# Edge stage: blocks of 128 edges as rows, VectorE adds the second operand, one transpose turns two blocks

## The reference, cut to what matters

```python
pair_emb = jnp.concatenate([node_emb[src], node_emb[dst]], axis=-1)
h = jax.nn.relu(pair_emb @ W1 + b1)
interaction = h @ W2 + b2
gate = jax.nn.sigmoid(interaction @ Wg + bg)
gated = interaction * gate
summed = jax.ops.segment_sum(gated, src, num_segments=N)
counts = jax.ops.segment_sum(jnp.ones((src.shape[0],), dtype=gated.dtype), src, num_segments=N)
pooled = summed / jnp.maximum(counts, 1.0)[:, None]
```

## Time and profile before

| | |
|---|---|
| median of three runs | 5001.01 us |
| profiled execution | 4962.42 us |
| its span, first to last instruction | 4960.7 us |
| granted TensorE clock, mean over the span | 0.797 |
| TensorE busy | 4009.5 us, 81% |
| VectorE, ScalarE, GpSimd busy | 44%, 35%, 32% |

### The profile page before, as it was taken

How to read it: one execution, slowest core, us unless ns; L and a number is a source line. 1 busy time by engine, 2 the same in 40 slices (tenths; PEclk the granted TensorE clock), 3 DMA queues, 4 the chain that set the end, 5 groups by cost and what they waited for, 6 DMA issues and landing times.

```text
span 4960.7 us, 126573 instructions
## 1 busy us (share of the span) xinstructions
PE 4009.5 (81%) x39351; PEld 3118.5 (63%) x39352; DVE 2186.5 (44%) x6634; ACT 1758.1 (35%) x3890; POOL 1586.5 (32%) x1694
## 2 busy tenths in 40 slices
PE   6872688888798999948888888888888888878786
PEld 3442344444598988937676667667667666766665
DVE  9998899999602111132222222222222222222224
ACT  7861588888400000122222222222222222222222
POOL 0000100000000000155555555555555555555553
PEclk9985899999899999967767776766766667677766
DMA  1000122222598888721111111111111111111111
GB/s 39 3 2 9 62 105 115 104 104 104 212 343 303 318 299 317 240 47 40 40 38 41 40 40 38 40 37 40 39 38 39 40 39 38 40 38 41 39 40 35
DMA packets 182862, 444.87 MB, mean 90 GB/s; under 512 B 52923, under 2 KB 111555, under 8 KB 156959
## 3 DMA queue, kind: packets, MB, share of 16 engines
q1 hardware_dynamic: 131503, 387.98, 22.8%
q0 software_dynamic: 51040, 53.55, 5.5%
q10 hardware_dynamic: 144, 1.05, 0.1%
HBM read 356.29 MB, written 86.12 MB: 89 GB/s over the span
## 4 chain that ended last, share of the span: by engine, by line
PE 53%; DVE 13%; another core or an unknown queue 11%; issue 10%; ACTq 6%; ACT 5%; DMA 1%; POOL 0%; DVEq 0%; SPq 0%; PEldq 0%; POOLq 0%
PE ps L1576 13%; PE ps L1726 9%; PE ps L1748 8%; PE ps L1736 8%; DVE x L558 8%; PE ps L1723 7%; PE ps L1550 6%; DVE rows L712 3%; ACTq L1385 2%; ACTq L1379 2%; ACTq L1384 2%; ACT stage L1306 2%; ACT ps L1290 1%; PE ps L1469 1%
## 5 line engine op out<-in xcount | busy, mean ns | idle before, releaser
L1089 POOL DMA_INDIRECT x<-b_table,gidx x1568 | 1486.6, 948 | 1273.9 <-ACT x L1387 767.0
L934 DVE TENSOR_TENSOR x<-x,ps 128x256 f32<-128x256 f32 x440 | 185.3, 421 | 1576.7 <-ACT x L1400 1415.4
L1394 ACT ACTIVATE x<-ps,b1col 64x512 f32<-64x512 f32 x440 | 298.6, 679 | 1517.3 <-remote 770.3
L1736 PE MATMUL ps<-w2cat,x 65*128 65x128 f32 x3520 | 682.7, 350 | 107.1 <-ACT x L1394 71.9
L1726 PEld LDWEIGHTS ps<-ident,x 128*64 128x64 f32 x3520 | 599.8, 186 | 230.8 <-issue 194.7
L1550 PE MATMUL ps<-rows 128*128 128x448 bf16 x2272 | 616.2, 400 | 148.2 <-DVE rows L712 69.6
L1726 PE MATMUL ps<-ident,x 128*64 128x128 f32 x3520 | 677.1, 351 | 69.3 <-issue 68.9
L1748 PE MATMUL ps<-x 128*128 128x65 f32 x3520 | 626.3, 337 | 114.9 <-DVE x L934 103.3
L1736 PEld LDWEIGHTS ps<-w2cat,x 65*128 65x128 f32 x3520 | 576.6, 247 | 224.2 <-issue 147.3
L1748 PEld LDWEIGHTS ps<-x 128*128 128x128 f32 x3520 | 600.1, 257 | 144.9 <-DVE x L934 135.0
L1723 PE MATMUL ps<-x 128*64 128x512 bf16 x1320 | 524.4, 522 | 184.9 <-issue 149.8
(11 more groups left out here) (271 smaller groups left out, 2610.0 us busy)
## 6 DMA issues: line engine op xcount, KB each, us to landing
rows<-adjacency SPq DMA_DIRECT2D x90, 1024.0 KB, 5.5
adjacency<-stage SPq DMA_DIRECT2D x50, 1568.0 KB, 5.2
x<-adjacency SPq DMA_DIRECT2D x60, 1024.0 KB, 5.7
x<-src_rows SPq DMA_DIRECT2D x440, 128.0 KB
rows<-adjacency SPq DMA_DIRECT2D x90, 544.0 KB, 4.7
x<-adjacency SPq DMA_DIRECT2D x60, 544.0 KB, 5.3
x<-b_table,gidx POOLq DMA_INDIRECT x1568
key_rows<-x ACTq DMA_DIRECT2D x1, 1024.0 KB, 4.3
```

The costliest lines, as they stand in the source:

```text
L1089: e.indirect_dma_start(out=BGT[:, s, j, :], out_offset=None, in_=b_table, in_offset=bass.IndirectOffsetOnAxis(ap=gidx[:, u * G + j:u * G + ...
L1736: ins = e.matmul(ps[:, 2 + u, j * P:(j + 1) * P], H[0:D + 1, u, j * P:(j + 1) * P], w2cat[:], start=True, stop=True)
```

## The change

The first product is turned around. For each block of 128 edges the one-hot matrix is now the stationary operand (128x128, bf16) and the A part moves (64 columns): 4 blocks by 3 parts make 12 products, and A[src] comes out with edges as rows, in bank 6 or 7. VectorE adds it to the gathered B in `BT`, in place (`add_b`). Then TensorE turns the sum with a transpose; one transpose takes 128 columns, that is two blocks of 64 features, and puts the even block on partitions 0 to 63 and the odd one on 64 to 127. ScalarE's rectifier becomes two instructions, one for each half of the partitions, and each writes every second block of `H`. b1 is loaded twice, one copy for each half.

The step of an item is cut in two (rows, turn), so interact and sum_edges come one step later, and VectorE's and ScalarE's orders change to fit. Steps that are written out ahead of the loop go from 4 to 8 items. The core of the diff:

```diff
-        b1col = sb("b1col", [D, 1], F32)
+        b1col = sb("b1col", [P, 1], F32)
...
                 if not first:
-                    e.wait_ge(h_ps_ready, i - 1)
+                    e.wait_ge(rows_ready, i - 1)
                 e.tensor_scalar(OT[:, s % 2, :], SROW[:, s, :], part_f[:, 0:1], None,
                                 ALU.is_equal).then_inc(ot_ready, 1)
+
+            def add_b(i, s):
+
+                e.wait_ge(rows_ready, i + 1)
+                e.wait_ge(b_copied, i + 1)
+                e.tensor_tensor(BT[:, s, :], ps[:, 6 + s % 2, 0:G * D], BT[:, s, :], ALU.add).then_inc(b_added, 1)
...
-            with e.Fori(1, ITEMS // 4) as r:
+            with e.Fori(2, ITEMS // 4) as r:
                 for s in range(4):
                     i = 4 * r + s
+                    add_b(i - 2, (s + 2) % 4)
                     make_hot_t(i, r, s, False)
-                    gated(i - 2, s % 2, False)
-                    add_sum(i - 3, (s + 1) % 2)
-                    make_hot(i, s, False)
+                    gated(i - 4, s % 2, False)
+                    add_sum(i - 5, (s + 1) % 2)
+                    make_hot(i - 1, (s + 3) % 4, False)
...
-            e.dma_start(b1col[:], b1.rearrange("(n a) -> n a", a=1)).then_inc(weights_in, 16)
+            for h in range(2):
+                e.dma_start(b1col[h * D:(h + 1) * D, :], b1.rearrange("(n a) -> n a", a=1)).then_inc(weights_in, 16)
...
-                e.activation(H[0:D, u, :], ps[0:D, u, :], ACT.Relu, bias=b1col[:, 0:1]).then_inc(h_ready, 1)
+                pair = H[0:D, u, :].rearrange("p (a h n) -> p a h n", h=2, n=P)
+                for h in range(2):
+                    ins = e.activation(pair[:, :, h, :],
+                                       ps[h * D:(h + 1) * D, u, 0:2 * P].rearrange("p (a n) -> p a n", n=P),
+                                       ACT.Relu, bias=b1col[h * D:(h + 1) * D, 0:1])
+                ins.then_inc(h_ready, 1)
...
-                    hidden(i, s % 2, False)
+                    hidden(i - 1, (s + 1) % 2, False)
+                    gate(i - 2, s % 2, False)
                     copy_part(i + 2, (s + 2) % 4, False)
-                    gate(i - 1, (s + 1) % 2, False)
...
-                for k in range(3):
-                    e.matmul(ps[0:D, u, :], AT[:, s, k * D:(k + 1) * D], OT[:, u, :], start=(k == 0), stop=False,
-                             skip_group_check=True)
-                for j in range(G):
-                    ins = e.matmul(ps[0:D, u, j * P:(j + 1) * P], BT[:, s, j * D:(j + 1) * D], ident[:], start=False,
-                                   stop=(j == G - 1), skip_group_check=True)
+                if not first:
+                    e.wait_ge(b_added, i - 1)
+                for j in range(G):
+                    for k in range(3):
+                        ins = e.matmul(ps[:, 6 + s % 2, j * D:(j + 1) * D], OT[:, s % 2, j * P:(j + 1) * P],
+                                       AT[:, s, k * D:(k + 1) * D], start=(k == 0), stop=(k == 2))
+                ins.then_inc(rows_ready, 1)
+
+            def turn_rows(i, s, first):
+
+                e.wait_ge(b_added, i + 1)
+                if not first:
+                    e.wait_ge(h_ready, i - 1)
+                e.sem_inc(turn_passed, 1)
+                for j in range(G // 2):
+                    ins = e.transpose(ps[:, s % 2, j * P:(j + 1) * P], BT[:, s, j * P:(j + 1) * P], ident[:])
                 ins.then_inc(h_ps_ready, 1)
...
-                    hidden(i, s, False)
-                    interact(i - 1, (s + 1) % 2, False)
-                    sum_edges(i - 2, (s + 2) % 4, False)
+                    edge_rows(i, s, False)
+                    turn_rows(i - 1, (s + 3) % 4, False)
+                    interact(i - 2, s % 2, False)
+                    sum_edges(i - 3, (s + 1) % 4, False)
```

More of the change, by code:

```diff
@@ L400, in build_gnn @@
         h_ps_ready = sem("h_ps_ready")
+        rows_ready = sem("rows_ready")
+        b_added = sem("b_added")
+        turn_passed = sem("turn_passed")
         h_ready = sem("h_ready")
@@ L1405, in _ @@
             copy_part(1, 1, True)
-            for i in range(4):
-                hidden(i, i % 2, i < 2)
+            for i in range(8):
+                if i >= 1:
+                    hidden(i - 1, (i - 1) % 2, i < 3)
+                if i >= 2:
+                    gate(i - 2, i % 2, i < 4)
                 copy_part(i + 2, (i + 2) % 4, i < 2)
-                if i:
-                    gate(i - 1, (i - 1) % 2, i < 3)
-            with e.Fori(1, ITEMS // 4) as rnd:
+            with e.Fori(2, ITEMS // 4) as rnd:
                 for s in range(4):
                     i = 4 * rnd + s
-                    hidden(i, s % 2, False)
+                    hidden(i - 1, (s + 1) % 2, False)
+                    gate(i - 2, s % 2, False)
                     copy_part(i + 2, (s + 2) % 4, False)
-                    gate(i - 1, (s + 1) % 2, False)
-            gate(ITEMS - 1, (ITEMS - 1) % 2, False)
+            hidden(ITEMS - 1, (ITEMS - 1) % 2, False)
+            for i in (ITEMS - 2, ITEMS - 1):
+                gate(i, i % 2, False)
             for half in range(2):
@@ L1426, in _ @@
             e.wait_ge(consts, 18)
-            e.wait_ge(weights_in, 16 * 22)
+            e.wait_ge(weights_in, 16 * 23)
             for n in range(4):
@@ L1711, in _, with edge_rows @@
                 pair_products(g, g % 4, 0)
[L1714 to L1716 removed]
+            def edge_rows(i, s, first):
                 e.wait_ge(at_ready, i + 1)
                 e.wait_ge(ot_ready, i + 1)
[L1719 removed]
+                if not first:
[7 more added lines that the diff above has]
+                e.wait_ge(b_added, i + 1)
                 if not first:
                     e.wait_ge(h_ready, i - 1)
[L1722 to L1727 removed]
+                e.sem_inc(turn_passed, 1)
+                for j in range(G // 2):
+                    ins = e.transpose(ps[:, s % 2, j * P:(j + 1) * P], BT[:, s, j * P:(j + 1) * P], ident[:])
                 ins.then_inc(h_ps_ready, 1)
```

43 lines of the change are left out of this document (25 added, 18 removed).

## The result

The changed kernel takes 5061.46 us in the median of four runs (5051.99 to 5064.45). The kernel before, run beside it, takes 5001.32 us (4997.68 to 5018.78). The ratio is 1.011, with a 95% interval from 1.0083 to 1.0137: slower by 1.1%. I had forecast 4490 us and a range from 4320 to 4690. Both the size and the sign are wrong.

The account below looks back on a forecast made before the run. TensorE's own work was taken to bound the edge stage, with GpSimd next. 2188 us outside it, 2262 for 440 items and 5 for the longer pipeline make 4455; plus 38.6 to the median, about 4490 us, range 4320 to 4690.

Parts of the forecast that it names:

- I carry this loss over as a share: Edge stage: 21% of the stage, lost to slowly issued TensorE matmuls, was taken to stay the same share after the change.
- I keep the share f = 0.40 and the 21% loss: Edge stage sum: full clock for 0.40 of the time and 21% lost, both unchanged, giving 5.14 us per item.
- TensorE's item: TensorE's work per edge-stage item: 5.31 us at half clock (saves 1.40), 2.84 us at full clock (saves 0.73).
- The clock: TensorE's granted clock in the edge stage: stays near 0.70, read as 2.4 GHz for 0.40 of the time, otherwise 1.2.
- VectorE: VectorE's edge-stage turn: the new addition takes 0.42 us, making the turn 2.9 us, up to 3.2.
- ScalarE: ScalarE's edge-stage turn: two rectifiers of 0.37 us each replace one of 0.68; turn 2.8 to 2.93 us, hidden.
- GpSimd is the next bound: GpSimd's 1568 gathers with issue gaps need 1989 us, so the edge stage can't get much shorter than that.
- Rival 1: TensorE's clock stays at 1.2 GHz nearly all the time: 5.6 us per item, about 4690 us; chance 22%.
- Rival 2: Full clock more often or fewer slow stretches, so GpSimd becomes the bound: about 4230 us; chance 19%.
- Rival 3: VectorE's addition is late each time and TensorE's turn waits for it: about 5790 us, slower; chance 4%.
- Rival 4: Weight loads of the 12 products don't overlap, 0.098 to 0.151 us each: about 4990 us, no change; chance 3%.
- Case 5: The lost 21% is a fixed 1.3 us per item: 5.23 us per item, 40 us above the sum; within the forecast's 50%.

Follow-up runs that it names:

- e1: Changed kernel with no gathers behind the first eight groups, GpSimd only signalling (later B wrong): 4159.34 us.
- e15: Changed kernel with a 128-column memset on GpSimd and a wait for its end behind every four gathers: 4709.46 us, 0.926 of the kernel before.
- e17: Kernel before with a short memset on GpSimd and a wait for its end behind every four gathers: 4708.89 us, ratio 1.1344 to the kernel before without it.
- e13: Changed kernel with a 0.70 us memset behind every four gathers, waiting only for the memset two groups back: 5030.04 us, 0.9893 of the kernel before.
- e18: Changed kernel with a four-column memset on GpSimd and a wait for its end behind every four gathers: 4666.5 us, ratio 1.125 to the kernel before.
- e7: Changed kernel with a 1024-column memset on GpSimd and a wait for its end behind every four gathers: 4998.21 us, 1.0001 of the kernel before.
- e5: Changed kernel with a 957 ns GpSimd memset in place of each gather after the first ring (later B wrong): 4257.95 us.

## Why the prediction was wrong, point by point

- **The step that failed** is "I carry this loss over as a share" with "I keep the share f = 0.40 and the 21% loss". Neither stayed as it was when the stream of work changed. The loss went from 21% to 32%, and the clock share from 0.40 to nothing. For the loss the runs show GpSimd's long rows of gathers in its place (e1, e15); why the new stream is held at half clock stays open.
- **TensorE's item** was forecast at 5.31 us at half clock and is 4.43. The 12 products cost 3510.65 - 3509.99 = 0.66 us (forecast 0.64). The two transposes are one matmul each, where the forecast took two, and cost 0.46 us in all (forecast 0.86 and 0.2 between groups). Interact and sum cost 3.31 us where I kept 3.61. Every error here was on the cautious side; a full-clock item never occurred.
- **The clock** alone, with the measured item and the loss at 21%, would give 440 x 4.43 / 0.79 = 2467 us, 4655 in all. Of the 5064 - 4455 = 609 us between the profiled execution and the forecast's own time, 4655 - 4455 = 200 are the clock's, with the shorter item set against it, and 5064 - 4655 = 409 are the loss's. So the loss is the greater part.
- **VectorE** was right: the addition takes 0.420 us, and L1758 waits for it 73.6 us in the whole stage. **ScalarE**'s two rectifiers take 0.467 us each in place of 0.37; hidden.
- **"GpSimd is the next bound"** was right as a floor and wrong as something apart from the 21%. The row that I had shows it: in the slow stretch of the earlier trace rows GpSimd was busy for 2.83 of 6.60 us while VectorE did nothing and TensorE 2.11. I read the windows for who released TensorE and not for who worked all the time. In the kernel before GpSimd paused often in the steady part; TensorE's timeline lies beside this of GpSimd's:

```profile
3462.97 0.95 POOL L1089 DMA_INDIRECT x<-b_table,gidx  x1 [0.30 <-issue]
3465.10 0.94 POOL L1089 DMA_INDIRECT x<-b_table,gidx  x1 [1.18 <-issue]
```

  and in front of the slow stretch of the earlier trace rows it ran on:

```profile
3515.41 0.94 POOL L1089 DMA_INDIRECT x<-b_table,gidx  x1 [4.28 <-ACT x L1387]
...
3524.16 0.94 POOL L1089 DMA_INDIRECT x<-b_table,gidx  x1 [0.30 <-issue]
```

- **Rival 1** (clock at 1.2 GHz) had the clock right and took the loss at 0.3 us an item, where it is 2.1. **Rival 2** (GpSimd bound, 4187 us own time) did not come in the result; in the last set the kernel before itself took 4148.58 us, so about this time was to be had without the change. **Rival 3** falls: 62 waits of turn(i-1), 73.6 us. **Rival 4** falls: a product each 0.66 / 12 = 0.055 us. **Case 5**, the loss as a fixed 1.3 us, was nearer the truth in kind, but the loss grew.

Put together, the change made each TensorE item 2.28 us shorter at half clock. It took the full clock away, which the old item had for 0.40 of the time. And GpSimd gathered on in longer rows, beside which 920 us were given back in slow issue.

## What to carry to other kernels

A loss that no engine causes in the profile is not a share to be kept: look which engine works without a pause just before it, and ask whether the change makes it work more. When GpSimd's gathers stand beside a stream of small matmuls, a short pause behind every few gathers is worth a trial (the changed kernel with it, e15, takes 7.4% less than the kernel before in a set where the stretches are there), but compare it in several sets, since in the last one the same pause made the kernel before 13% slower (e17). The granted clock of a new stream is to be measured and not carried over from the old one.

## What the runs showed of the hardware that was not expected

- Beside 8 or more gathers in a row (0.95 us each, 1.25 us apart) TensorE issues an instruction mostly only every 0.7 us or a multiple of it, in most stretches of the changed kernel from 6 to 8 us after the first gather until 1 to 4 us after the last. A pause of 1.64 us behind every four gathers stops it (e15), 0.87 us does not (e13). What in the gathering does it is open, and so is why the last set was without it.
- A gather behind a memset and a wait for its end starts 1.42 us after that end, whatever the memset's size (0.12, 0.22 and 0.98 us in e18, e15 and e7). Behind a memset two groups back it is 0.17 us (e13), and a memset behind such a wait starts after 0.15 us (e5), so it is not the wait alone.
- Memsets of 0.95 us on GpSimd made VectorE's float32 one-hots (128x128) 0.82 us long in e5, where they take 0.28 in e1.
- TensorE busy for 400 of 400 us was granted 0.50 with the new item, with or without transposes and with 12 or 4 bf16 products, and 1.00 with the old item.
- The same kernel on one core, with runs within 0.4% of each other, took 4149 us in one set and 4991 to 5089 in the others, two of these sets under the same chip number.
